# Expert blocks of 256 rows of one expert, and a first product whose stationary operand is the weight

## The reference

```
x = x + 0.5 * ffn(layernorm(x))        # stage 1: phases A and B of layer 0
x = x + attn(layernorm(x))             # Fourier attention, a cumulative sum over the sequence
x = x + 0.5 * ffn(layernorm(x))        # phases A and B of layer 1

ffn(xf):
    shared = silu(xf @ sw1) * (xf @ sw3) @ sw2             # every token
    s = sigmoid(xf @ router_w.T); two best of 8 experts; gates from s
    h = gelu(xf @ ew1[e]); y = h @ ew2[e]                  # e: each of the token's two experts
    out = shared + sum over its two experts of gate * y
```

## Time and profile before

| | us |
|---|---|
| median of 3 runs | 2051.76 |
| the profiled execution | 2060.44 |
| its span | 2058.6 |
| PE busy | 1597.5 |
| DVE busy | 1419.2 |
| POOL busy | 766.7 |
| ACT busy | 672.2 |

### The profile page before, as it was taken

One profiled execution on the slowest core, in us unless ns is written; L12 is line 12 of the kernel. 1 busy time (PEld: TensorE's weight loads), 2 busy tenths in 40 slices (PEclk: granted clock), 3 DMA queues, 4 the chain that ended last, 5 costly groups with the idle time before them and its releaser, 6 DMA issues.

```text
span 2058.6 us, 35171 instructions
## 1 busy us (share of the span) xinstructions
PE 1597.5 (78%) x9854; PEld 1381.3 (67%) x9855; DVE 1419.2 (69%) x3362; ACT 672.2 (33%) x1126; POOL 766.7 (37%) x868
## 2 busy tenths in 40 slices
PE   2899999589999466767767674489999976999940
PEld 1777777489999355555555563377777766999940
DVE  4788888545555368888898888377788763555557
ACT  3334343134444133232323131233433412444410
POOL 0444444225454223333333232044444432555420
PEclk9999999889999767776777676599999987999975
DMA  8211111144444301010101000011111114444459
GB/s 276 82 53 42 55 50 47 53 120 143 140 142 135 96 22 41 21 41 20 41 20 41 20 20 0 31 54 51 45 50 55 42 44 114 140 138 143 136 194 349
DMA packets 123782, 170.36 MB, mean 83 GB/s; under 512 B 14881, under 2 KB 105394, under 8 KB 123442
## 3 DMA queue, kind: packets, MB, share of 16 engines
q1 hardware_dynamic: 89938, 91.05, 15.5%
q0 software_dynamic: 25344, 70.29, 9.3%
q10 hardware_dynamic: 8448, 8.39, 1.2%
HBM read 91.03 MB, written 81.89 MB: 84 GB/s over the span
## 4 chain that ended last, share of the span: by engine, by line
PE 47%; DVE 18%; issue 12%; DMA 10%; POOL 7%; ACT 3%; SPq 2%; POOLq 0%; DVEq 0%; ACTq 0%
PE bank L613 14%; PE bank L614 12%; PE bank L615 12%; POOL lists L407 6%; DMA lists<-a_rows,a_slots 5%; PE bank L739 3%; PE bank L749 3%; DVE t_rn L1149 2%; DMA f_yf<-results 2%; DVE t_cum L1167 2%; ACT a_rows L503 2%; DVE a_gate_u L987 1%; PE bank L843 1%; DVE X L1230 1%; DVE t_pr L1165 1%
## 5 line engine op out<-in xcount | busy, mean ns | idle before, releaser
L418 POOL DMA_INDIRECT results<-b_yb,b_goal x272 | 261.6, 962 | 343.6 <-DVE b_yb L1090 298.4
L407 POOL DMA_INDIRECT lists<-a_rows,a_slots x256 | 259.8, 1015 | 117.5 <-issue 64.5
L613 PE MATMUL bank<-t_xah,t_wfh 128*128 128x512 f32 x192 | 115.0, 599 | 113.6 <-DVE t_xal L864 64.1
L1090 DVE COPY b_yb<-bank 128x512 f32<-128x512 f32 x136 | 94.0, 691 | 147.9 <-PE bank L615 147.9
L613 PE MATMUL bank<-a_sw2h,a_uh 128*128 128x256 f32 x512 | 155.4, 304 | 42.7 <-DVE a_xtl L864 35.7
L613 PE MATMUL bank<-ew_h,b_xbth 128*128 x544 | 166.7, 306 | 1.1 <-DVE b_xbtl L864 1.0
L613 PE MATMUL bank<-ew_h,b_hth 128*128 x544 | 155.9, 287 | 7.5 <-DVE b_htl L864 3.0
L457 ACT ACTIVATE a_uh<-a_gate_u 128x512 fp32r<-128x512 f32 x128 | 77.1, 624 | 245.9 <-PE bank L615 193.0
L614 PE MATMUL bank<-ew_l,b_xbth 128*128 x544 | 154.1, 283 | 0.0
L615 PE MATMUL bank<-ew_h,b_xbtl 128*128 x544 | 153.8, 283 | 0.0
L615 PE MATMUL bank<-ew_h,b_htl 128*128 x544 | 152.4, 280 | 0.0
(11 more groups left out here) (212 smaller groups left out, 4882.2 us busy)
## 6 DMA issues: line engine op xcount, KB each, us to landing
b_xb<-lists SPq DMA_DIRECT2D x272, 132.0 KB
t_yg<-results SPq DMA_DIRECT2D x32, 512.0 KB, 4.6
f_yf<-results SPq DMA_DIRECT2D x32, 512.0 KB, 10.9
X<-in_L_attn_x SPq DMA_DIRECT2D x16, 512.0 KB, 4.1
out<-X ACTq DMA_DIRECT2D x16, 512.0 KB, 7.1
results<-b_yb,b_goal POOLq DMA_INDIRECT x272
w_raw_ew<-in_L_ffn_ew SPq DMA_DIRECT2D x2, 2048.0 KB, 13.8
lists<-a_rows,a_slots POOLq DMA_INDIRECT x256, 2.4
```

The lines of the kernel that those rows point to most:

```text
L407: pool.indirect_dma_start(out=lists, out_offset=bass.IndirectOffsetOnAxis(ap=slots[:, q, k, j:j + 1], axis=0), in_=rows[:, q, j, :], in_of ...
L418: pool.indirect_dma_start(out=results, out_offset=bass.IndirectOffsetOnAxis(ap=goal[:, slot, blk:blk + 1], axis=0), in_=YB[:, slot, blk, : ...
L613: pe.matmul(o, a("h"), b("h"), start=first, stop=False)
L1090: dve.tensor_copy(YB[:, slot].rearrange("p b d -> p (b d)"), bank[:, 7 - par, :]).then_inc(s_yok, 1)
```

## The change

The blocks become twice as long. A block has BR = 256 rows, all of one expert, and each step takes one block. The number of steps a layer is PAIRS = (2 * 8192 + 8 * 255) // 256 = 71, which is enough for any counts; it was 68. The list of an expert is now filled up with 256 rows, and SP loads a block with one DMA of 256 rows.

With one expert in a step, the first product can be turned round: the weight `W1` (128 x 128 pieces) is stationary and the 256 transposed rows are streamed. Its result is the hidden layer already transposed, as the second product needs it. The four transposes of `HB` go, and `HT` is made from `HB` in SBUF. The stationary operand is read at a fixed address: before each step ACT copies the high part, and DVE the low part, of that expert's `ew1` (128 x 512 numbers each) to `W1`, double buffered; each reads the expert's number from the table with `value_load`. The second product is as before but with one expert a step.

The low part of `HT` is now made in the step of its own block, behind the row part and the weight copy, and ahead of the copy to `YB`; it was made a step later, at the start.

```diff
-BLOCKS = TOPK * TILES + E
-PAIRS = BLOCKS // 2
+PAIRS = (TOPK * TOKENS + E * (BR - 1)) // BR
...
@@ SP
-                    for blk in range(2):
-                        row = sp.value_load(table[0:1, bass.ds(n * 2 + blk, 1)], min_val=0,
-                        sp.dma_start(XB[:, slot, blk, :], lists[bass.ds(row, P), :]).then_inc(s_xb[slot], 16)
+                    row = sp.value_load(table[0:1, bass.ds(n, 1)], min_val=0, max_val=E * CAP + SPARE - BR)
+                    sp.dma_start(XB[:, slot, :, :],
+                                 lists[bass.ds(row, BR), :].rearrange("(b p) r -> p b r", p=P)).then_inc(s_xb[slot], 16)
...
@@ ACT
-                    if inside(s - 1, PAIRS):
-                        act.wait_ge(s_hT, s + p0)
-                        copy(HT["h"][:, 1 - par].rearrange("p k b t -> p (k b t)"),
-                             bank[:, 4 + 1 - par, :]).then_inc(s_hh, 1)
...
+                        e = act.value_load(table[0:1, bass.ds(s + (PAIRS + 1), 1)], min_val=0, max_val=E - 1)
+                        atleast(act, s_mm1, s + p0)
+                        copy(W1["h"][:, 1 - par], EW[1, "h"][:].rearrange("p (e n) -> p e n", e=E)[:, bass.ds(e, 1), :]
+                             .rearrange("p a n -> p (a n)")).then_inc(s_w1h, 1)
...
+                        act.activation(HB[:, par], bank[:, 2 + par, :], ACT.Gelu).then_inc(s_gelu, 1)
+                        act.wait_ge(s_gelu, s + (p0 + 1))
+                        atleast(act, s_yps, s + (p0 - 1))
+                        copy(HT["h"][:, par].rearrange("p m t -> p (m t)"), HB[:, par]).then_inc(s_hh, 1)
...
@@ PE
-                    if inside(s - 1, PAIRS):
-                        pe.wait_ge(s_gelu, s + p0)
-                        atleast(pe, s_hl, s + (p0 - 2))
-                        for k in range(KD):
-                            for blk in range(2):
-                                ins = pe.transpose(bank[:, 5 - par, (2 * k + blk) * P:(2 * k + blk + 1) * P],
-                                                   HB[:, 1 - par, blk, k * P:(k + 1) * P], ident)
-                        ins.then_inc(s_hT, 1)
...
+                        pe.wait_ge(s_w1h, s + (p0 + 1))
+                        pe.wait_ge(s_w1l, s + (p0 + 1))
                         atleast(pe, s_gelu, s + (p0 - 1))
-                        for blk in range(2):
+                        for m in range(KD):
                             for k in range(KD):
-                                ins = three(bank[:, 2 + par, blk * HR:(blk + 1) * HR],
-                                            lambda h: XBT[h][:, par, k, blk, :],
-                                            lambda h: expert(1, h, at[blk], k), k == 0, k == KD - 1)
+                                ins = three(bank[:, 2 + par, m * BR:(m + 1) * BR],
+                                            lambda h: W1[h][:, par, k * HR + m * P:k * HR + (m + 1) * P],
+                                            lambda h: XBT[h][:, par, k].rearrange("p b t -> p (b t)"),
+                                            k == 0, k == KD - 1)
...
@@ DVE
-                    if inside(s - 1, PAIRS):
-                        dve.wait_ge(s_hh, s + p0)
-                        low(HT["l"][:, 1 - par].rearrange(flat), bank[:, 5 - par, :],
-                            HT["h"][:, 1 - par].rearrange(flat)).then_inc(s_hl, 1)
...
+                        e = dve.value_load(table[0:1, bass.ds(s + (PAIRS + 1), 1)], min_val=0, max_val=E - 1)
+                        atleast(dve, s_mm1, s + p0)
+                        dve.tensor_copy(W1["l"][:, 1 - par], EW[1, "l"][:].rearrange("p (e n) -> p e n", e=E)
+                                        [:, bass.ds(e, 1), :].rearrange("p a n -> p (a n)")).then_inc(s_w1l, 1)
+                    if inside(s, PAIRS):
+                        dve.wait_ge(s_hh, s + (p0 + 1))
+                        low(HT["l"][:, par].rearrange("p m t -> p (m t)"), HB[:, par],
+                            HT["h"][:, par].rearrange("p m t -> p (m t)")).then_inc(s_hl, 1)
```

More of the change, by code:

```diff
@@ L42 @@
 HR = 256
-CAP = TOKENS + P
+BR = 2 * P
+CAP = TOKENS + BR
 ROW = D + 8
-BLOCKS = TOPK * TILES + E
-PAIRS = BLOCKS // 2
+PAIRS = (TOPK * TOKENS + E * (BR - 1)) // BR
+FULL = TOKENS // BR
+SPARE = E * BR
+TURNS = [(PAIRS - i + 3) // 4 for i in range(4)]
 LN_EPS, FFT_EPS, GATE_EPS = 1e-5, 1e-8, 1e-9
@@ L154, in build @@
         carry = sb("carry", [P, E], F32)
-        table = sb("table", [1, 2 * BLOCKS + E], I32)
+        table = sb("table", [1, 2 * PAIRS + E], I32)
         st = sb("st", [P, 2, J, 6], F32)
@@ L744, in step @@
                         turn = q if u < 3 else q + 1
-                        pe.wait_ge(s_xb[slot], turn * 32 + (YW * layer + 32))
+                        pe.wait_ge(s_xb[slot], turn * 16 + (YW[slot] // 2 * layer + 16))
                         atleast(pe, s_bl, s + p0)
@@ L771, in step @@
                         for blk in range(2):
-                            for k in range(KD):
+                            for m in range(KD):
                                 ins = three(bank[:, 7 - par, blk * D:(blk + 1) * D],
-                                            lambda h: HT[h][:, 1 - par, k, blk, :],
-                                            lambda h: expert(2, h, at[blk], k), k == 0, k == KD - 1)
+                                            lambda h: HT[h][:, 1 - par, m, blk * P:(blk + 1) * P],
+                                            lambda h: expert(2, h, before, m * HR, HR), m == 0, m == KD - 1)
                         ins.then_inc(s_yps, 1)
                 pe.wait_ge(s_table, layer + 1)
-                offset = [[pe.alloc_register(f"expert_{layer}_{par}_{blk}") for blk in range(2)] for par in range(2)]
-                run_steps(pe, step, -1, 4, PAIRS - 4, PAIRS + 1, 4)
+                offset = [pe.alloc_register(f"expert_{layer}_{par}") for par in range(2)]
+                run_steps(pe, step, -1, 4, PAIRS - 3, PAIRS + 1, 4)
             def attention_weights():
@@ L1070, in phase_b @@
                 p0 = PAIRS * layer
+                dve.wait_ge(s_table, layer + 1)
                 def step(s, u, q):
@@ L1081, in step @@
                         turn = q if u < 3 else q + 1
-                        atleast(dve, s_ysc[slot], turn * 32 + YW * layer)
+                        atleast(dve, s_ysc[slot], turn * 32 + YW[slot] * layer)
                         dve.wait_ge(s_bh, s + (p0 + 2))
```

86 lines of the change are left out of this document (41 added, 45 removed).

## The result

The changed kernel takes 2088.43 us (median of four, 2086.85 to 2090.93), the kernel before 2051.24 beside it: ratio 1.0179, with a 95% interval of 1.0159 to 1.0199, 37.2 us slower. The forecast was 2067, 15 us slower.

What follows compares the result with a forecast made beforehand. PE was taken to bound phase B before, a ring of waits after: 71 x 3.76 less 256.4 less 3.2 gives +7.4 us a layer, +14.7 in two, so 2066.5 us against the median; 8-in-10 range 2030 to 2105.

Steps and rivals of the forecast that it cites:

- the ring: Phase B: `YB` copy, POOL's two DMAs, landing, `goal` four blocks on, next `YB` copy; 7.51 us per two steps, 3.76 a step.
- PE's need without the hidden transposes: Phase B: PE's step falls from 3.69 by 0.44 to 3.25 us, or 3.33 with the turn of the unrolled loop.
- `goal` to `YB`: DVE's stretch in a phase B step: 0.08 + 0.78 + 0.34 + 0.61 = 1.81 us, ends 1.64 and 2.16, before 0.69.
- `YB` to `goal`: Phase B, results' DMAs and landing: 5.36 to 6.16 us, middle 5.70 if early and late landings alternate.
- 68 steps at 256.4 us: Phase B before the change, a layer: 68 steps of 3.77 us, taken as 256.4 us.
- `block_table`: Serial table passes ahead of phase B: they halve, 3.2 us less a layer.
- Filling: Eight filling DMAs, twice as long: between nothing and 4.2 us more a layer, taken as nothing.
- ACT and the clock at nothing: Phase B: ACT's 2.4 to 3.3 us a step add nothing; granted clock stays 1.00, its fall (2385 us) having chance 0.03.
- POOL's DMA under DVE's instructions: Phase B: `b_w1l` or `b_htl` under way when POOL's DMA starts costs up to 0.57 us in two steps.
- the long ring: Slower rival, phase B: held-up POOL DMAs or late landings throughout give some 4.0 us a step, 2101 us; chance 0.29.
- the second rival: Phase B: late landings throughout, (1.81 + 6.16) / 2 = 3.99 us a step, or stretched POOL DMAs; 2101 us, chance 0.29.
- the break-even step of 3.66: Phase B step at which the change would neither gain nor lose: (256.4 + 3.2) / 71 = 3.66 us.

Runs made afterwards that it cites:

- a_two_goals: Changed kernel, destination numbers copied early to a second tile, `goal` copy and its landing wait two steps later, rolled loop from step 8: 1990.64 us, 0.9715 of the kernel before.
- a_w1l_act: Changed kernel with the low part of `W1` copied by ACT instead of DVE, which reads no table: 2052.22 us, 1.0002 of the kernel before.
- a_fixed_again: Changed kernel without DVE's table read, always copying the first expert's low part of the weight: 2072.99 us, 1.0102 of the kernel before.

## Why the prediction was wrong in size

The direction, the ring, its members and the place of the new waits were as forecast; the sum of +15 us was less than half of the 37. Of the signs it named, the step (3.97, not 3.76) failed, and `goal` waited in nearly every block of one ring and in half of the other's. By its own steps:

- **PE's need without the hidden transposes**, 3.25, or 3.33 with the loop's turn: right. `a_two_goals`, where PE alone binds, takes 3.29.
- **`goal` to `YB`**, 1.81 us: measured 1.85 and 1.86 in single turns, 1.94 on the mean. On the mean the reading of the table, taken at 0.78, is 0.87 from the start of the low part, and the weight copy, taken at 0.34, is 0.39 (0.83 and 0.34 in the single turn above). The 0.13 too little make 0.065 a step, 9 us in all 142 steps.
- **`YB` to `goal`, "the middle being 5.70 if early and late landings go on taking turns"**: this is the step that failed. They do take turns, from block to block; but blocks of one parity form a ring for themselves, and the landings of the other don't shorten it. A mean over both would be right for one ring that meets each in turn. Here the ring with the late landing sets the pace, at 6.02 and 5.93, and the early one waits. 0.28 more in two steps is 0.14 a step, 20 us in all. The two together: (1.94 + 5.98) / 2 = 3.96 in place of 3.76.
- **68 steps at 256.4 us**: their mean step was 3.795 and not 3.77, so 258.1. Phase B also has a beginning and an end that go by other times; from the first `goal` to the last `YB` copy before, 6.2 and 7.9 us stood beside the 68 steps, and 1.8 and 3.3 beside the 71 now. That gives back 4.5 a layer, of which 1.8 lie between the first `goal` and the first `YB` copy (10.8 before, 9.0 now). The forecast had no term for it.
- **`block_table`** -3.2: measured -2.9. **Filling** 0: no more issue time, as taken, and 1.0 us until it has landed.
- **ACT and the clock at nothing**: right. The granted clock was 1.00 from 437 to 683 us, and DVE's low part of `HT` waits for ACT's copy in the early ring, which has the time, and hardly in the late one (3 of 58 blocks).
- **POOL's DMA under DVE's instructions**: priced in the long ring at up to 0.57 in two steps. In single blocks the DMAs did grow by that much, 0.13 us a turn on the mean of the slower ring, and most of it didn't reach the landing leg. The Trainium skill, page "SBUF — State Buffer", says in the section "SBUF: two separate sides" that whichever of the two starts first has the shared port for the whole instruction. The trace agrees but for the first moments: all long DMAs began under `b_w1l` or `b_htl`, and none of the 118 that were already under way when such an instruction began was (two rows below); but 22 that the profile has begin up to 0.05 us behind the start of such an instruction took 0.96 too, and there the DVE instruction was the longer one (`b_htl` 0.73 to 0.77 us in place of 0.69, `b_w1l` 0.49 to 0.51 in place of 0.43).

```profile
543.03 0.96 POOL L421 DMA_INDIRECT results<-b_yb,b_goal  x1 [2.44 <-DVE b_yb L1092]
```

```profile
543.04 0.45 DVE L1083 CAST b_w1l<-ew_l 128x512 fp32r x1
```

The sum by layers, measured: steps 71 x 3.97 - 68 x 3.795 = +23.8; beginning and end -4.5; `block_table` and filling -2.3 from the first of its passes shown to the first `goal` (-2.0 in layer 1); +17.0, and twice that +34. The medians say +37.2. The 3 us that are left are not accounted for; single executions differ by more than that in stages that the change doesn't touch: from the last `YB` copy of layer 0 to `block_table` of layer 1 the trace of after is 11.5 us shorter than that of before.

So what came true is the arithmetic of the second rival, late landings throughout, 3.99 a step; it had a chance of 0.29 for reasons of which one, the late landing, held for one ring in two, and one is enough. Two errors of the forecast also worked against each other, since the break-even step of 3.66 was too low: `a_w1l_act`, at 3.73, takes the time of the kernel before (1.0002), and with the terms as measured it is (258.1 + 4.5 + 2.3) / 71 = 3.73; the forecast's step of 3.76 would have cost some 4 us, not 15.

What stays open: what settles which parity becomes the late one; how much of the late landing is left when no loads run beside it, since they were halved and not taken out; and why one of the chips takes 1.6% more for the kernel before.

## What to carry to other kernels

Where a wait spans several steps, write the ring down with its step count and see whether it is one ring or several side by side; with several, add up the legs of each by itself and let the slowest set the pace, never a mean over all; the same holds for anything that lengthens a leg. A wait for a buffer to come free belongs as late in its engine's order as its first reader allows, and what else has to be early is copied out first: here a tile of eight numbers a partition and the moving of one wait turned a loss of 1.8% into a gain of 2.8%. When a change makes the bounding engine shorter, the next bound was hidden and its length is not known from the profile beyond its single legs; a kernel that moves the wait out of the way is worth a run before the change is given up.

## What the runs showed of the hardware that was not expected

- Reading a number from a table in SBUF on DVE and using it as an address takes until 0.83 us after the start of the instruction ahead, 0.23 more than that instruction itself takes up (0.60, `a_fixed_again`).
- DMAs of 128 rows to `results` landed 0.5 to 0.6 us later in the ring whose landings meet row loads of 264 KB (6.02 and 5.93 us from the `YB` copy, for 5.40 and 5.46), and 0.2 later with the loads halved.
- An indirect DMA on POOL grew from 0.96 to up to 1.45 us when it began more than 0.05 us into `b_w1l` or `b_htl`, DVE's instructions with their operands in SBUF, by what was left of the instruction less 0.12 us. When it began before such an instruction or in its first 0.05 us it didn't grow. The other way round, `b_w1l` took 0.49 to 0.66 us in place of 0.43 in the 23 cases where it began 0.5 to 0.7 us into such a DMA.
- One chip took 2084.20 us for the kernel before where three others took 2049.42 to 2052.51; comparisons were therefore made only within a chip.
